# Three kernel buffers instead of two in the PSUM of a dynamic-convolution stage, with the other users moved together

## What is computed

```python
enh  = conv3x3_depthwise(conv1x1(x, w_conv1_pw), w_conv1_dw)
h1, h2 = split(conv3x3_grouped(x, w_conv2_g))
attn = conv1x1(h1 * h2, w_conv2_pw) * attgamma + conv1x1(x, w_conv211)      # 16 coefficients per pixel
# a 3x3 kernel for each pixel and group of 2 channels, mixed from 16 sets:
attk = einsum('bpn,nm->bpm', attn, selfw).reshape(B, P, 64, 2, 18)
y    = einsum('bpgij,bpgj->bpgi', attk, patches_3x3(enh)) + attn @ selfb
out  = y * ga1 + enh + x
```

## Time and profile before

| | |
|---|---|
| runs | 5519.98 us median of 3 (5519.8 to 5520.31) |
| profiled execution | 5518.02 us, of which the span of the trace is 5515.9 us |
| layer 0 and set-up | to about 1880 us |
| convolution stage | from there to the end, 64 bands |
| busy over the span | PE 97%, DVE 93%, POOL 77%, PEld 71%, ACT 60% |
| granted TensorE clock | 0.99 to 1.00 of full speed in nearly every slice |

### The profile page before, as it was taken

The page is one execution under the profiler, slowest core; times in us unless marked ns, Lnnn a source line. Parts: engine busy times, 40 slices in busy tenths (PEclk is TensorE's granted clock), DMA queues, the critical chain, the costliest instruction groups (busy, mean ns, idle before and its releaser), DMA issues.

```text
span 5515.9 us, 112725 instructions
## 1 busy us (share of the span) xinstructions
PE 5377.8 (97%) x37904; PEld 3907.0 (71%) x37904; DVE 5149.3 (93%) x5424; ACT 3324.5 (60%) x4094; POOL 4237.7 (77%) x1958
## 2 busy tenths in 40 slices
PE   8999999999999799999999999999999999999998
PEld 7888888888888466666666666666666666666666
DVE  7888888888888699999999999999999999999999
ACT  6888888888888554555555554555555554555553
POOL 4655565556555688888888888888888888888886
PEclk9999999999999899999999999999999999999999
DMA  3222222222222222222222222222222222222221
GB/s 92 74 76 76 71 74 76 76 71 73 76 76 68 78 71 83 69 79 74 73 81 73 79 71 81 69 79 73 72 81 73 79 72 81 70 80 72 72 81 47
DMA packets 175616, 413.21 MB, mean 75 GB/s; under 512 B 37201, under 2 KB 58769, under 8 KB 175505
## 3 DMA queue, kind: packets, MB, share of 16 engines
q1 hardware_dynamic: 175568, 412.59, 24.5%
HBM read 228.94 MB, written 145.77 MB: 68 GB/s over the span
## 4 chain that ended last, share of the span: by engine, by line
PE 48%; DVE 12%; issue 5%; POOL 1%; DVEq 0%; ACT 0%; POOLq 0%
PE ps_k L1035 18%; PE ps_t L1055 15%; PE ps_m L1017 9%; DVE products L1259 6%; PE ps_p L994 3%; DVE products L1265 3%; DVE ps_k L1259 2%; PE ps_t L1067 2%; PE ps_t L1065 1%; POOL enh L953 1%; DVE h_prod L1279 1%; DVEq L133 0%; DVEq L1252 0%; DVEq L1277 0%; PE ps_t L994 0%
## 5 line engine op out<-in xcount | busy, mean ns | idle before, releaser
L953 POOL TENSOR_TENSOR enh<-enh,tap 128x1024 f32<-128x1024 f32 x1024 | 2263.0, 2210 | 68.0 <-ACT tap L1174 9.3
L1259 DVE TENSOR_TENSOR products<-ps_k,enh 128x1024 f32<-128x1024 f32 x1664 | 1997.7, 1218 | 53.3 <-PE ps_k L1035 39.6
L1035 PE MATMUL ps_k<-att,basis 128*128 128x512 f32 x4608 | 1682.8, 449 | 80.6 <-DVE products L1265 56.5
L1174 ACT ACTIVATE tap<-e,dw 128x1024 f32<-128x1024 f32 x1024 | 1147.5, 1146 | 313.2 <-POOL enh L953 312.0
L486 POOL TENSOR_TENSOR hidden_lo<-hidden,hidden_hi 128x1024 fp32r<-128x1024 f32 x256 | 693.3, 2729 | 717.5 <-DVE hidden_hi L691 717.5
L959 POOL TENSOR_TENSOR products<-products 128x1024 f32<-128x1024 f32 x384 | 915.9, 2392 | 418.2 <-DVE products L1259 418.2
L1035 PEld LDWEIGHTS ps_k<-att,basis 128*128 128x128 f32 x4608 | 707.1, 189 | 689.7 <-DVE products L1259 409.7
L1265 DVE TENSOR_TENSOR products<-ps_k,products 128x1024 f32<-128x1024 f32 x640 | 783.7, 1225 | 21.8
L1259 DVE TENSOR_TENSOR ps_k<-ps_k,enh 128x1024 f32<-128x1024 f32 x640 | 784.5, 1226 | 20.5 <-PE ps_k L1035 3.8
L1055 PE MATMUL ps_t<-ident_swap,products 128*128 128x128 f32 x5120 | 736.6, 272 | 0.7 <-POOL products L959 0.7
L1055 PE MATMUL ps_t<-ident,products 128*128 128x128 f32 x5120 | 724.9, 272 | 0.1
(11 more groups left out here) (115 smaller groups left out, 7273.9 us busy)
## 6 DMA issues: line engine op xcount, KB each, us to landing
xin<-layer_out SPq DMA_DIRECT2D x64, 1280.0 KB, 7.3
xt<-in_x SPq DMA_DIRECT2D x128, 512.0 KB, 4.1
layer_out<-xo SPq DMA_DIRECT2D x128, 512.0 KB, 2.9
x_own<-layer_out SPq DMA_DIRECT2D x128, 512.0 KB, 4.0
out<-out_sb SPq DMA_DIRECT2D x256, 256.0 KB, 2.0
att<-att_hi SPq DMA_DIRECT2D x512, 32.0 KB, 2.0
att<-att_lo SPq DMA_DIRECT2D x512, 32.0 KB, 2.0
enh<-edge_rows SPq DMA_DIRECT2D x64, 130.0 KB, 2.1
```

The lines of the kernel that those rows point to most:

```text
L953: nc.gpsimd.tensor_tensor(own, own, tap_sb[add % TAP_BUFFERS][:, 0:hi - lo, :], ALU.add).then_inc(dw_done, 1)
L1035: mm = nc.tensor.matmul(ps_k[KERNEL_BUFFER[q] ^ (SWAPPED & p)][:, BANK * s:BANK * (s + 1)], basis[:, 2 * t + s, :], att[p][:, j, :], start ...
L1174: nc.scalar.activation(tap_sb[add % TAP_BUFFERS][:, 0:hi - lo, :], src, ACT.Copy, scale=dw[:, t:t + 1]).then_inc(tap_ready, 1)
L1259: nc.vector.tensor_tensor(out, kernels, enh[p][:, r:r + CHUNK_ROWS, dx:dx + W].unsqueeze(1).to_broadcast([C, 2, CHUNK_ROWS, W]), ALU.mult) ...
```

## The change

A third buffer ps_k is added (six banks). The four chunk sums and their back transposes share one bank ps_t, and projection, convolution and coefficients share ps_m. So a chunk's first half now waits for the copy of the chunk before (`out_ready` of j, not j - 1), the projection waits for att_lo, and the convolution for the last e0 copy. All slots are given anew, one merge moves from q 15 to 16, GpSimd's merges, ScalarE's taps and SyncE's issues are reordered. SyncE's order in a step becomes load_own(n, 0), move_h2(m), loads(l), store(o, 3), load_own(n, 1), attention_rows(m), keep_edge(n), fetch_edge(m), store(n, 0), (n, 1), (n, 2). The matmuls, products, transposes, copies and DMAs of a band stay the same in number and shape. The diff, cut:

```diff
-VECTOR_MERGES = (2, 6, 9, 11, 15, 18, 22, 27, 31, 33)
+VECTOR_MERGES = (2, 6, 9, 11, 16, 18, 22, 27, 31, 33)
-KERNEL_BUFFER = {0: 0, 1: 1}
-for q in range(2, Q):
-    KERNEL_BUFFER[q] = KERNEL_BUFFER[FREEING[q - 2][1]]
-SWAPPED = KERNEL_BUFFER[FREEING[-2][1]]
-KERNEL_FREE = {q: FREEING[q - 2][0] if q >= 2 else FREEING[q - 2][0] - SLOTS_IN_BAND for q in range(Q)}
+KERNEL_BUFFERS = 3
+KERNEL_BUFFER = {q: q for q in range(KERNEL_BUFFERS)}
+for q in range(KERNEL_BUFFERS, Q):
+    KERNEL_BUFFER[q] = KERNEL_BUFFER[FREEING[q - KERNEL_BUFFERS][1]]
+KERNEL_FREE = {q: FREEING[q - KERNEL_BUFFERS][0] - (SLOTS_IN_BAND if q < KERNEL_BUFFERS else 0) for q in range(Q)}
...
-HALF_SLOT = {0: 10, 1: 7, 6: 6, 7: 6, 8: 11, 9: 9, 14: 11, 15: 11, 16: 12, 17: 12, 20: 15, 21: 19, 24: 15, 25: 18, 26: 25, 27: 25, 32: 22, 33: 22, 34: 22, 35: 22, 38: 26, 39: 28, 40: 31, 41: 31, 46: 33, 47: 32, 48: 37, 49: 37, 52: 35, 53: 35, 56: 38, 57: 38, 58: 44, 59: 44, 64: 44, 65: 43, 68: 47, 69: 48, 70: 47, 71: 47}
+HALF_SLOT = {6: 7, 7: 6, 0: 9, 1: 8, 14: 11, 15: 9, 16: 12, 17: 11, 8: 8, 9: 14, 20: 21, 21: 21, 24: 17, 25: 17, 30: 19, 31: 21, 34: 24, 35: 21, 26: 23, 27: 23, 38: 31, 39: 36, 46: 30, 47: 30, 40: 38, 41: 32, 52: 35, 53: 33, 48: 36, 49: 39, 56: 48, 57: 45, 64: 45, 65: 44, 58: 44, 59: 46, 68: 47, 69: 49, 70: 47, 71: 48}
-X_SLOTS = [16, 25, 38, 48]
+X_SLOTS = [14, 25, 39, 49]
-BACK_SLOTS = [21, 34, 40, 51]
+BACK_SLOTS = [15, 28, 42, 51]
-POOL_MERGE_PLACES = (0, 0.6000000000000001, 3.0, 6.0, 9.5, 10.9)
+POOL_MERGE_PLACES = (0.5, 1, 5.0, 10.5, 11.5, 13.9)
-TAP_PLACES = ((0.5, 1.5, 3.0, 5.5, 10.5, 13.0, 13.5, 14.0, 19.5), (22.0, 24.5, 27.0, 28.0, 31.0, 35.5, 36.5, 36.5, 41.5))
-CLEAR_PLACE = 64
+TAP_PLACES = ((0.0, 0.0, 0.0, 1.0, 5.0, 11.0, 12.0, 13.5, 14.0), (17.5, 18.5, 22.0, 22.5, 29.5, 32.0, 32.5, 33.5, 38.4))
+CLEAR_PLACE = 62
-H_PROD_SLOT = 27
-ATT_HIGH = 28
-ATT_LOW = 33
-CONV_SLOTS = [33, 33, 42, 42, 42, 42, 46, 46, 50, 50, 54, 54, 59, 59, 59, 59, 66, 66]
-COEFFICIENT_SLOT = 28
-PW_SLOTS = [17, 19, 27, 30, 36]
+H_PROD_SLOT = 8
+ATT_HIGH = 12
+ATT_LOW = 12
+CONV_SLOTS = [24, 24, 27, 27, 27, 27, 33, 33, 33, 33, 37, 37, 42, 42, 42, 42, 46, 46]
+COEFFICIENT_SLOT = 7
+PW_SLOTS = [14, 15, 17, 19, 22]
...
-        ps_k = [bank(f"ps_k{i}", 2) for i in range(2)]
-        ps_t = [bank(f"ps_t{i}") for i in range(2)]
-        ps_p = bank("ps_p")
+        ps_k = [bank(f"ps_k{i}", 2) for i in range(KERNEL_BUFFERS)]
+        ps_t = bank("ps_t")
         ps_m = bank("ps_m")
-        first_banks = [ps_p, ps_t[0], ps_t[1], ps_p, ps_t[0]]
+        first_banks = [ps_k[2][:, 0:BANK], ps_k[2][:, BANK:2 * BANK], ps_t, ps_k[2][:, 0:BANK], ps_k[2][:, BANK:2 * BANK]]
...
                         pe.wait_ge(e0_ready, PW_CHUNKS * m + c)
+                        if c == 0:
+                            pe.wait_ge(att_lo_ready, m)
...
-                            at_least(pe, att_lo_ready, m)
+                            if not isinstance(m, int) or m > 0:
+                                pe.wait_ge(e0_ready, PW_CHUNKS * m + PW_CHUNKS)
...
                     if start:
-                        at_least(pe, out_ready, CHUNKS * n + j - 1)
+                        at_least(pe, out_ready, CHUNKS * n + j)
...
-                        mm = nc.tensor.matmul(ps_t[j % 2][:, C * r:C * (r + 1)], rows, (ident, ident_swap)[s][:, :], is_transpose=True,
+                        mm = nc.tensor.matmul(ps_t[:, C * r:C * (r + 1)], rows, (ident, ident_swap)[s][:, :], is_transpose=True,
```

More of the change, by code:

```diff
@@ L92 @@
 POOL_TERM_COUNT = {q: i + 1 for i, q in enumerate(sorted(POOL_MERGES, key=LAST_HALF.get))}
-BACK_SLOTS = [21, 34, 40, 51]
+BACK_SLOTS = [15, 28, 42, 51]
 POOL_PLACES = 2 * (TAPS - 1)
-POOL_MERGE_PLACES = (0, 0.6000000000000001, 3.0, 6.0, 9.5, 10.9)
-TAP_PLACES = ((0.5, 1.5, 3.0, 5.5, 10.5, 13.0, 13.5, 14.0, 19.5), (22.0, 24.5, 27.0, 28.0, 31.0, 35.5, 36.5, 36.5, 41.5))
-CLEAR_PLACE = 64
-H_PROD_SLOT = 27
-ATT_HIGH = 28
-ATT_LOW = 33
-CONV_SLOTS = [33, 33, 42, 42, 42, 42, 46, 46, 50, 50, 54, 54, 59, 59, 59, 59, 66, 66]
-COEFFICIENT_SLOT = 28
-PW_SLOTS = [17, 19, 27, 30, 36]
+POOL_MERGE_PLACES = (0.5, 1, 5.0, 10.5, 11.5, 13.9)
[7 more added lines that the diff above has]
+PW_SLOTS = [14, 15, 17, 19, 22]
+assert all(HALVES_OF[j][0][0] > BACK_SLOTS[j - 1] for j in range(1, CHUNKS)) and HALVES_OF[0][0][0] + SLOTS_IN_BAND > BACK_SLOTS[-1]
+assert all(BACK_SLOTS[j] > HALVES_OF[j][-1][0] for j in range(CHUNKS))
+assert PW_SLOTS[-1] < CONV_SLOTS[0] and SLOTS_IN_BAND <= CONV_SLOTS[-1] <= COEFFICIENT_SLOT + SLOTS_IN_BAND and COEFFICIENT_SLOT <= PW_SLOTS[0]
+assert BACK_SLOTS[-1] - SLOTS_IN_BAND < COEFFICIENT_SLOT
 def at_least(engine, semaphore, value):
@@ L909, in step @@
                         load_own(n, 0)
+                    if m is not None:
+                        move_h2(m)
+                    if l is not None and not (isinstance(l, int) and l == 0):
+                        loads(l, p)
                     if o is not None:
                         store(o, CHUNKS - 1)
-                    if l is not None and not (isinstance(l, int) and l == 0):
-                        loads(l, p)
                     if n is not None:
                         load_own(n, 1)
[L916 to L923, removed]
                     if m is not None:
@@ L928, in step @@
                         fetch_edge(m, b)
+                    if n is not None and not (isinstance(n, int) and n == bands - 1):
+                        keep_edge(n, p)
+                    if m is not None and not (isinstance(m, int) and m == 0):
+                        fetch_edge(m, b)
                     if n is not None:
+                        store(n, 0)
                         store(n, 1)
@@ L990, in pointwise @@
                         pe.wait_ge(e0_ready, PW_CHUNKS * m + c)
-                    elif c > first_banks.index(first_banks[c]):
-                        pe.wait_ge(e0_ready, first_banks.index(first_banks[c]) + 1)
+                        if c == 0:
+                            pe.wait_ge(att_lo_ready, m)
+                    elif c >= 3:
+                        pe.wait_ge(e0_ready, c - 2)
                     lo, hi = PAD + CHUNK_ROWS * c, min(PAD + CHUNK_ROWS * (c + 1), XROWS)
-                    nc.tensor.matmul((first_banks[c] if first else ps_p)[:, 0:W * (hi - lo)], pwT[:, :], xin[p][:, lo:hi, 1:W + 1],
+                    nc.tensor.matmul((first_banks[c] if first else ps_m)[:, 0:W * (hi - lo)], pwT[:, :], xin[p][:, lo:hi, 1:W + 1],
                                      start=True, stop=True).then_inc(pw_done, 1)
@@ L1064, in back @@
                     pe.wait_ge(sumT_ready, CHUNKS * n + j + 1)
-                    nc.tensor.matmul(ps_t[j % 2][:, :], basis[:, SLOTS - 1, :], att[p][:, j, :], start=True, stop=False, skip_group_check=True)
+                    nc.tensor.matmul(ps_t[:, :], basis[:, SLOTS - 1, :], att[p][:, j, :], start=True, stop=False, skip_group_check=True)
                     for r in range(CHUNK_ROWS):
-                        mm = nc.tensor.matmul(ps_t[j % 2][:, C * r:C * (r + 1)], summedT[j % 2][:, C * r:C * (r + 1)], ident[:, :],
+                        mm = nc.tensor.matmul(ps_t[:, C * r:C * (r + 1)], summedT[j % 2][:, C * r:C * (r + 1)], ident[:, :],
                                               is_transpose=True, start=False, stop=(r == CHUNK_ROWS - 1), skip_group_check=True)
@@ L1117, in e0_rows @@
                     lo, hi = PAD + CHUNK_ROWS * c, min(PAD + CHUNK_ROWS * (c + 1), XROWS)
-                    ps = (first_banks[c] if isinstance(m, int) and m == 0 else ps_p)[:, 0:W * (hi - lo)]
+                    ps = (first_banks[c] if isinstance(m, int) and m == 0 else ps_m)[:, 0:W * (hi - lo)]
                     nc.scalar.activation(e0[p][:, lo:hi, 1:W + 1], ps.rearrange("c (h w) -> c h w", w=W), ACT.Identity,
@@ L1148, in sum_out @@
                     at_least(act, back_done, CHUNKS * n + j - 1)
-                    nc.scalar.activation(summedT[j % 2][:, :], ps_t[j % 2][:, :], ACT.Copy).then_inc(sumT_ready, 1)
+                    nc.scalar.activation(summedT[j % 2][:, :], ps_t[:, :], ACT.Copy).then_inc(sumT_ready, 1)
                 def chunk_out(n, j):
```

10 lines of the change are left out of this document (6 added, 4 removed).

## The result

The changed kernel takes 5424.7 us (median of four runs, 5423.44 to 5425.26), the kernel before 5520.15 (5519.8 to 5521.32): a ratio of 0.9826, 95% interval 0.9809 to 0.9843. It is 95 us faster; the forecast was 5432 in a range of 5400 to 5500. The profiled execution took 5425.26 us with a span of 5423.2.

A forecast was written before the change was run, and what follows sets the result against it. VectorE and TensorE were taken to wait for each other through a two-deep ring. The period would fall from 56.39 to 54.8, with 0.2 allowed 55.0; 1.39 x 63 = 88 us off gives 5432 us, range 5400 to 5500.

The forecast's parts named there:

- ring of two: Two kernel buffers between TensorE and VectorE: TensorE work over some 0.3 us before kernels makes VectorE wait, 1.71 us a band.
- The sum: TensorE's queue from slot 13 to the next step's slot 4, then VectorE to operation 13: period 54.8 us.
- leftover: VectorE's remaining wait at operation 7, which TensorE's queue frees at 46.63 and VectorE wants at 46.32: about 0.3 us.
- The allowance of 0.2: Added to the period for varying pieces in the stretch without slack, giving 55.0 us a band.
- Start and end: First projections go to the free third buffer and nothing there is longer: zero.
- The eighth trip: Last ps_t output copy, slots 5 to 6: open by 0.43 us, in a stretch with 1.5 to spare, costed at nothing.
- the seven that were called covered: The other ps_t copy trips, 0.94 or 0.90 us each, hidden behind other TensorE work, four of them just.
- Rivals A and C: A (20%): two thin covers meet tap products, 5495 us. C (8%): single ps_t opens its trips, slower, 5637 or 5565.
- Rivals B and D: B (7%): third buffer empty, TensorE's load near 56, 5499 us. D (10%): VectorE's floor reached, 5398 us.
- the sum of pieces: TensorE's own work per band, added from kernels, transposes, taps and projections: 53.6 us before, 53.3 after.
- VectorE's floor of 54.45: VectorE's band without waits, from distances between starts, after h_prod and att_lo moved: 54.45 us, 54.68 before.
- The stretch from slot 13 to slot 4: TensorE's queue from the kernels of q 13 to slot 4's, 44.55 us without slack, never waiting for VectorE.

The follow-up runs named there:

- five-piece kernels: Changed kernel with five convolution pieces instead of six: double pieces at slots 27 and 37, 5455.08 us; first double piece at slot 26 instead, 5454.49 us.
- late merges: Changed kernel with six of VectorE's ten merges issued one product later: 5423.55 us.
- moved groups: Changed kernel with TensorE groups moved forward into its waits of slots 12 to 16, nothing added or taken out: 5409.88 us.
- the double piece at slot 37: Changed kernel with five convolution pieces, double ones at slots 26 and 37: 5454.49 us; with six merges later and groups moved forward as well, 5456.98 us.
- the versions without a visible pause: Changed kernel with a three-tap convolution piece at slot 26, 5412.26 us; changed kernel with groups moved forward into slots 12 to 16, 5409.88 us.

## Why the prediction was right

- **The bound before.** The prediction had VectorE and TensorE each waiting for the other through a ring of two, with 1.71 us a band lost to bursts. Two runs support it: the new order on two buffers (+404 us), and six pieces in the old order (+40 us with less work on TensorE). After the change 54.81 - 54.45 = 0.36 of the 1.71 is left.
- **The period.** The sum gave 54.8, the trace 54.81. Its leftover was 0.3 us; it measured 0.42, at operations 6 and 7, where operation 7 was named.
- **The allowance of 0.2** for what the sum leaves out, 12.6 us in all, was not needed for the period. It is most of why 5432 stands above 5424.7.
- **Start and end, costed at zero,** was wrong: 7.6 us, from the convolution that now stands in front of the first kernels. The rows that I had read the earlier trace rows gave only the steady period. The allowance too much and the start too little cancel in part, so part of the closeness is luck.
- **The single ps_t.** The eighth trip is open in slots with time to spare: its wait shows as 0.22 and costs nothing visible. Of the seven that were called covered, two show a weight-load wait of 0.2 and nothing in the matmuls, so they were covered, two of them just. That an uncovered one costs about its length in the stretch was shown (0.44 for 0.47). Rivals A and C fall: no wait for a sum's copy is longer than 0.3, so no whole tap product stood in the way.
- **Rivals B and D.** The total of TensorE was not near 56, since the period is 54.81; the sum of pieces (53.3 after the change) had said so. VectorE's floor of 54.45 was not reached, and in the changed kernel 0.69 less of its own work gained nothing.
- **The stretch from slot 13 to slot 4** was right as an amount and wrong as a picture. I took it for one sum in which TensorE never waits for VectorE. The trace shows it held by VectorE again at slots 15 and 21, by less than a tenth each, and the five-piece kernels show that sums from later slots bind as soon as work is moved behind them. By its own signs ("waits that I have costed at nothing") the prediction was wrong on this point; it was small here, some 0.2 us in 44.7. My expectations for the five-piece kernels failed where I used the single sum.
- **The rule of the Trainium skill** (Perfetto Trace Analysis, Optimizing Tensor Performance, Matmuls) that groups should rotate through banks so that copies overlap: the runs agree with its mechanism (28 us for one copy left uncovered). Where other banks' work as long as the trip stood in between, the matmuls show no wait; a second ps_t beside three buffers was not run.

What stays open: how much of the 1.58 us a band comes from depth alone and how much from the new order (which by the prediction's sums takes 0.34 off TensorE and 0.23 off VectorE), why the late merges and moved groups gain nothing with the double piece at slot 37, and the last 0.1 us between 54.6 and VectorE's floor in the versions without a visible pause.

## What to carry to other kernels

When two engines both look 98% busy and pass work through a ring of two, add up the pieces of each from starts, not from busy shares; if both sums are under the period, a burst in front of the ring is a likely cause and a deeper ring worth a trial. With the deeper ring, check the slower engine's queue from every point where it waits for the other, not only over the whole period: work saved before such a point is lost, work added behind it is paid. A shared bank cost here only the part of its round trip that had no other work in front (0.44 us for 0.47). An operation moved later on one engine can make the next one want its input sooner: count the distance between making and wanting again, not only the work saved.

## What the runs showed that I had not expected

- Less work can be slower, with either depth: minus 0.34 us a band on TensorE gave +40 us with two buffers and +30 us with three, by position alone.
- A convolution piece of three taps takes 2.80 us, of two 1.94, of one 1.07: 0.87 a tap and a fixed 0.2, beside the 0.20 on the kernels behind it. Pieces are worth joining only while the kernels' ring can bridge them: three buffers bridged 2.80 us in one order and not in another, where one product stood an operation earlier.
